# Maxima spread over the partitions by TensorE, and the projections' weights prepared apart for q, k and v

## What is computed

```python
x = x + _layernorm(attn(_layernorm(x)) )      # attn: qkv = x @ w_qkv.T + b_qkv, then per chunk:
    inter = jnp.einsum('bhcd,bhde->bhce', qb * decay_q[None, :, :, None], S)
    scores = jnp.einsum('bhcd,bhed->bhce', qb, kb) * dmask[None]
    intra = jnp.einsum('bhce,bhed->bhcd', scores, vb)
    S_new = lam_c[None, :, None, None] * S + jnp.einsum('bhcd,bhce->bhde', kb * decay_k[None, :, :, None], vb)
    # output: attn @ w_out.T + b_out
x = x + _layernorm(ffn(_layernorm(x)))        # ffn: wq = w.astype(float8_e4m3fn), y = (x @ wq) * scale
    gate = jax.nn.silu(_quantized_matmul(x, gate_w, gate_scale))
    up = _quantized_matmul(x, up_w, up_scale)
    y = _quantized_matmul(gate * up, down_w, down_scale)
```

## Time and profile before

| | us |
|---|---|
| median of 3 runs | 1037.26 |
| lowest, highest | 1037.1, 1037.28 |
| the profiled execution | 1037.88 |
| its span | 1036.1 |

### The profile page before, as it was taken

One profiled execution on the slowest core, in us unless ns is written; L12 is line 12 of the kernel. 1 busy time (PEld: TensorE's weight loads), 2 busy tenths in 40 slices (PEclk: granted clock), 3 DMA queues, 4 the chain that ended last, 5 costly groups with the idle time before them and its releaser, 6 DMA issues.

```text
span 1036.1 us, 21805 instructions
## 1 busy us (share of the span) xinstructions
PE 955.5 (92%) x8388; PEld 704.4 (68%) x8388; DVE 664.6 (64%) x1340; ACT 526.3 (51%) x997; POOL 686.2 (66%) x839
## 2 busy tenths in 40 slices
PE   1997988949988699999999999999999999999997
PEld 1775766636766486777867768677776787867774
DVE  7756767636478776666667656676666666666422
ACT  3535756535745563555635546355553555635432
POOL 2649898946765685676856768567585675856643
PEclk9998999979999899999999999999999999999999
DMA  9577989996899997494774947859477494732010
GB/s 342 142 208 196 253 203 254 214 266 180 192 194 225 204 195 143 113 184 89 147 146 110 183 88 149 152 104 184 91 145 140 115 184 94 144 69 42 26 37 21
DMA packets 297496, 159.79 MB, mean 154 GB/s; under 512 B 141616, under 2 KB 272688, under 8 KB 297264
## 3 DMA queue, kind: packets, MB, share of 16 engines
q1 hardware_dynamic: 296672, 157.86, 68.7%
q10 hardware_dynamic: 720, 0.54, 0.2%
HBM read 82.86 MB, written 41.94 MB: 120 GB/s over the span
## 4 chain that ended last, share of the span: by engine, by line
PE 48%; POOL 27%; DVE 8%; issue 8%; ACT 3%; SPq 2%; DMA 2%; POOLq 0%; DVEq 0%; ACTq 0%
PE bank L821 16%; PE bank L807 13%; PE att L784 8%; POOL att_pool L958 5%; POOL w_pool L972 4%; POOL hl L968 3%; POOL rstd L899 3%; PE bank L700 3%; PE bank L715 2%; POOL xr L964 2%; POOL rstd L903 2%; DVE stats L1206 2%; POOL vv L942 2%; DMA dram_qk<-qk_hl 2%; PE att L700 2%
## 5 line engine op out<-in xcount | busy, mean ns | idle before, releaser
L807 PE MATMUL bank<-f_pool,gate_q 128*128 128x256 f16 x1536 | 185.0, 274 | 5.4 <-DMA f_pool<-hl 4.4
L807 PE MATMUL bank<-f_pool,up_q 128*128 128x256 f16 x1536 | 183.4, 273 | 0.0
L821 PE MATMUL bank<-down_q,w_pool 128*128 128x512 f16 x768 | 168.3, 379 | 8.4 <-POOL w_pool L972 8.4
L958 POOL TENSOR_TENSOR att_pool<-p,att_pool 128x512 f16<-128x512 f32 x128 | 145.9, 1161 | 37.3 <-ACT att_pool L505 37.3
L807 PEld LDWEIGHTS bank<-f_pool,gate_q 128*128 128x128 f16 x1536 | 147.9, 98 | 26.3 <-DMA f_pool<-hl 4.6
L1337 DVE SCALAR_TENSOR_TENSOR w_pool<-bank,us_t,w_pool 128x256 f32<-128x256 f32 x192 | 84.0, 479 | 125.7 <-PE bank L807 100.1
L807 PEld LDWEIGHTS bank<-f_pool,up_q 128*128 128x128 f16 x1536 | 150.3, 98 | 17.5
L896 POOL TENSOR_TENSOR rstd<-mv,eps_t 128x1 f32<-128x1 f32 (+1 forms) x112 | 27.8, 249 | 192.4 <-DVE mv L1209 173.5
L821 PEld LDWEIGHTS bank<-down_q,w_pool 128*128 128x128 f16 x768 | 74.0, 98 | 96.7 <-issue 9.8
L972 POOL TENSOR_TENSOR w_pool<-w_pool 128x512 f16<-128x512 f32 x96 | 111.2, 1160 | 42.1 <-ACT w_pool L557 42.1
L505 ACT CAST att_pool<-p 128x512 f16<-128x512 f32 x128 | 76.7, 619 | 66.0 <-DVE p L1247 65.9
(11 more groups left out here) (139 smaller groups left out, 1800.1 us busy)
## 6 DMA issues: line engine op xcount, KB each, us to landing
xr<-in_x SPq DMA_DIRECT2D x32, 512.0 KB, 4.5
dram_qk<-qk_hl SPq DMA_DIRECT2D x64, 256.0 KB, 5.1
att_pool<-dram_qk SPq DMA_DIRECT2D x64, 256.0 KB, 6.8
f_pool<-dram_qk SPq DMA_DIRECT2D x64, 256.0 KB, 6.9
dram_v<-vv SPq DMA_DIRECT2D x32, 256.0 KB, 2.6
dram_kd<-kd_hl SPq DMA_DIRECT2D x32, 256.0 KB, 3.2
qn_pool<-dram_qk SPq DMA_DIRECT2D x32, 256.0 KB, 7.9
out_x<-w_pool SPq DMA_DIRECT2D x32, 256.0 KB, 2.1
```

The lines of the kernel that those rows point to most:

```text
L807: ins = nc.tensor.matmul(b[:, j * TOK:(j + 1) * TOK], w[:, k, o * P:(o + 1) * P], x1_hl[:, v % 2, part, k], start=(k == 0 and part == 0), ...
L821: ins = nc.tensor.matmul((b_gate, b_up)[t][:, :], h_hl[:, part, k, t * P:(t + 1) * P], down_q[:, k], start=(k == 0 and part == 0), stop=(k ...
L958: nc.gpsimd.tensor_tensor(pr_hl[:, 1, heads(g)], by_head(p32[:, g % 2]), pr_hl[:, 0, heads(g)], ALU.subtract).then_inc(p_lo_d, 1)
```

## The change

- **Loads.** x of unit 0 comes as two tiles with a semaphore each. The weights come by thirds (q, k, v; all four row blocks of 512 columns) in place of four row blocks of all columns; x of unit 1 follows the first third. The scale of the down projection is loaded by SP in `ahead(0)` and not by ACT's queue. An identity matrix (`eye_c`, float32) is a new input, in the memory of `state`; the ones lie in that of `state_d`.
- **Weights.** Bound, scale, bias and the two halves are made for each third apart. `third(w, part, half)` now takes all row blocks and 256 columns, the columns of one `project_qk(0, i)`, which waits for its own half.
- **Maxima.** POOL's two `partition_all_reduce` are gone. PE multiplies one column of maxima, broadcast over 128 columns, by the identity, so every partition has all 128 values, and DVE reduces them. For k and v these matmuls stand behind `project_qk(0, 0)` and `project_qk(0, 1)`.
- **Bound on the rows.** The 12 squares on ACT and 36 matmuls of ones are gone. DVE takes the largest absolute value of each row of a piece as it is rounded (`row_limit`), squares and adds 12 columns once (`row_sums`), and PE adds over partitions with one matmul (`sum_rows`). `norms` and `scale_h` run later: `scale_h` behind `ahead(13)`.
- **Unit loads.** `load_unit` has four steps, dealt out by `UNIT_STEPS`: unit 0 over `ahead(6)` to `ahead(9)`, unit 1 over `ahead(11)` to `ahead(13)`.

```diff
-        SUMMED = {3: (0,), 4: (1,), 5: (2,), 6: (3,), 7: (4,), 8: (5, 6), 9: (7,), 10: (8,), 11: (9,), 12: (10,),
-                  13: (11,)}
-        NORMS = {7: 0, 10: 1}
+
+        UNIT_STEPS = {6: ((0, 0),), 7: ((0, 1),), 8: ((0, 2),), 9: ((0, 3),),
+                      11: ((1, 0),), 12: ((1, 1), (1, 2)), 13: ((1, 3),)}
...
-            def load_unit(s):
+            def may_load(s):
...
+            def load_unit(s, step=None):
+                if step in (None, 0):
+                    may_load(s)
+                    load_stack(s, 1, (0, 0, 1, 1))
+                if step in (None, 1):
+                    load_stack(s, 0, (0, 1, 0, 1))
+                if step in (None, 2):
+                    load_q(s)
+                    load_v(s)
+                if step in (None, 3):
+                    load_kt(s)
...
                     sp.dma_start(bo[:, :], b_out).then_inc(wout_in, 16)
+                    sp.dma_start(ds_t[:, :], down_s).then_inc(scl_in, 16)
...
-            load_x(0)
-            for k in range(KT):
-                sp.dma_start(w_stage[:, k], w_qkv_t[k * P:(k + 1) * P, :]).then_inc(w_in[k], 16)
-            load_x(1)
+            for t in range(T):
+                sp.dma_start(xr[:, 0, t], x_u[0][:, t]).then_inc(x0_in[t], 16)
+            for part in range(3):
+                sp.dma_start(w_stage[:, :, part * D:(part + 1) * D],
+                             w_qkv_t.rearrange("(k p) n -> p k n", p=P)[:, :, part * D:(part + 1) * D]
+                             ).then_inc(w_in[part], 16)
+                if part == 0:
+                    load_x(1)
...
-                if k == LEAD - 6:
-                    load_unit(0)
-                if k == LEAD - 1:
-                    load_unit(1)
+                if k in UNIT_STEPS:
+                    for unit, step in UNIT_STEPS[k]:
+                        load_unit(unit, step)
...
-            def square(n):
-                act.wait_ge(f_q_d, n + 1)
-                at_least(act, square_mm, n - 1)
-                nc.scalar.activation(squares(n), piece_out(n), ACT.Square, scale=SQUARE).then_inc(square_d, 1)
...
-            act.dma_start(ds_t[:, :], down_s).then_inc(scl_in, 16)
-            x_normalise(0)
-            x_hi(0)
-            act.wait_ge(w_scale_d, 1)
-            for part in range(3):
-                for half in range(2):
-                    w_hi(third(wqkv_hi, part, half), third(w_stage, part, half))
+            for t in range(T):
+                act.wait_ge(rs_d[LN_X], t + 1)
+                normalised(LN_X, x_src(0)[:, t], x_src(0)[:, t], t).then_inc(nrm_d[LN_X], 1)
+                act.wait_ge(nrm_d[LN_X], t + 1)
+                nc.scalar.copy(x_half(0)[:, t, 0], x_src(0)[:, t]).then_inc(x_hi_d, 1)
+            w_hi(0)
             x_normalise(1)
             x_hi(1)
+            w_hi(1)
+            w_hi(2)
...
-                if 2 <= k < 14:
-                    square(k - 2)
...
-            def sum_squares(n):
-                pe.wait_ge(square_d, n + 1)
-                if n == 0:
-                    pe.wait_ge(eps_d, 3)
-                if n == 8:
-                    pe.wait_ge(norms_d, 1)
-                for k in range(3):
-                    ins = nc.tensor.matmul((b_gate, b_up)[n // 4 % 2][:, :], ones[:, :], squares(n)[:, k * D:(k + 1) * D],
-                                           start=(n % 4 == 0 and k == 0), stop=(n % 4 == 3 and k == 2))
-                ins.then_inc(square_mm, 1)
+            def sum_rows():
+                pe.wait_ge(eps_d, 3)
+                pe.wait_ge(row_sum_d, 1)
+                nc.tensor.matmul(b_gate[:, 0:4], ones, row_sum[:, :], start=True, stop=True).then_inc(row_sum_mm, 1)
+
+            def spread(out, col):
+                return nc.tensor.matmul(out, small[:, col:col + 1].to_broadcast([P, P]), eye, start=True, stop=True)
+
+            def spread_w_max(part):
+                pe.wait_ge(eye_in, 16)
+                pe.wait_ge(w_max, part + 1)
+                spread(b_gate[:, part * P:(part + 1) * P], part).then_inc(w_max_all, 1)
+
+            def spread_wout_max():
+                pe.wait_ge(wout_max, 1)
+                for n in range(3):
+                    ins = spread(b_up[:, n * P:(n + 1) * P], 20 + n)
+                ins.then_inc(wout_max_all, 1)
...
-                        if n == 0 and j == 0 and (i == 0 and k % 2 == 0 or i == 2 and k == 0):
-                            pe.wait_ge(w_lo_d, i + k // 2 + 1 if i == 0 else 4)
+                        if n == 0 and j == 0 and k == 0:
+                            pe.wait_ge(w_lo_d, i + 1)
...
+                if k == 2:
+                    spread_wout_max()
                 project_qk(k, 0)
+                if k == 0:
+                    spread_w_max(1)
                 project_qk(k, 1)
+                if k == 0:
+                    spread_w_max(2)
                 project_qk(k, 2)
                 project_qk(k, 3)
-                for n in SUMMED.get(k, ()):
-                    sum_squares(n)
+                if k == 12:
+                    sum_rows()
...
+            spread_w_max(0)
...
-            pool.wait_ge(w_max, 1)
-            nc.gpsimd.partition_all_reduce(small[:, 6:7], small[:, 5:6], P, RMAX).then_inc(w_max_all, 1)
...
-                if k == 1:
-                    pool.wait_ge(wout_max, 1)
-                    nc.gpsimd.partition_all_reduce(small[:, 36:39], small[:, 20:23], P, RMAX
-                                                   ).then_inc(wout_max_all, 1)
-                if k == 11:
+                if k == 12:
...
             def prepare_qkv():
...
+                                                 apply_absolute_value=True))
+                link(nc.vector.tensor_scalar(col(7, 3), col(4, 3), 1.0 / 256.0, None, ALU.mult))
+                w_limit(0, 0)
+                w_limit(0, 1)
+                x_moments(1, 0)
+                w_scale(0)
+                x_moments(1, 1)
+                scale_bias(0)
+                w_lo(0, 0)
+                w_lo(0, 1)
+                w_limit(1, 0)
+                w_limit(1, 1)
+                w_limit(2, 0)
+                w_scale(1)
+                w_limit(2, 1)
+                scale_bias(1)
+                w_lo(1, 0)
+                w_lo(1, 1)
+                w_scale(2)
+                scale_bias(2)
+                w_lo(2, 0)
+                w_lo(2, 1)
...
+            def w_limit(part, half):
+                dve.wait_ge(w_in[part], 16)
+                link(nc.vector.tensor_reduce(col(30 + 2 * part + half), w_stage[:, 2 * half:2 * half + 2,
+                                                                                part * D:(part + 1) * D],
+                                             AX.XY, ALU.max, apply_absolute_value=True))
+                if half:
+                    nc.vector.scalar_tensor_tensor(out=col(part), in0=col(30 + 2 * part), scalar=col(31 + 2 * part),
+                                                   in1=col(7 + part), op0=ALU.max, op1=ALU.max).then_inc(w_max, 1)
+
+            def w_scale(part):
+                dve.wait_ge(w_max_all, part + 1)
+                link(nc.vector.tensor_reduce(col(40 + part), b_gate[:, part * P:(part + 1) * P], AX.X, ALU.max))
+                power_of_two(col(43 + part), col(40 + part), 2.0 ** -30, 2.0 ** 35)
+                link(nc.vector.tensor_scalar(col(46 + part), col(43 + part), 2.0 ** -5, None, ALU.mult))
+                nc.vector.reciprocal(col(60 + part), col(46 + part)).then_inc(w_scale_d, 1)
...
 
             def scale_wout():
                 dve.wait_ge(wout_max_all, 1)
+                link(nc.vector.tensor_reduce(col(36, 3), b_up[:, 0:3 * P].rearrange("p (n q) -> p n q", n=3), AX.X,
+                                             ALU.max))
...
+            def row_limit(n):
+                dve.wait_ge(f_q_d, n + 1)
+                ins = nc.vector.tensor_reduce(row_max[:, n:n + 1], piece_out(n), AX.X, ALU.max,
+                                              apply_absolute_value=True)
+                ins.then_inc(row_max_d, 1)
+
+            def row_sums():
+                dve.wait_ge(row_max_d, 12)
+                link(nc.vector.tensor_reduce(col(24), row_max[:, :], AX.X, ALU.max))
+                link(nc.vector.tensor_scalar(col(25), col(24), E4M3_OVER, 0.0, ALU.mult, ALU.mult))
+                link(nc.vector.tensor_tensor(row_max[:, 0:8], row_max[:, 0:8], row_max[:, 0:8], ALU.mult))
+                link(nc.vector.tensor_reduce(row_sum[:, 0:2], row_max[:, 0:8].rearrange("p (w k) -> p w k", w=2), AX.X,
+                                             ALU.add))
+                nc.vector.tensor_scalar(row_sum[:, 2:4], row_sum[:, 0:2], 0.0, col(25), ALU.mult, ALU.add
+                                        ).then_inc(row_sum_d, 1)
+
+            def norms():
+                dve.wait_ge(row_sum_mm, 1)
+                nc.vector.tensor_scalar(col(26, 4), b_gate[:, 0:4], 1.0, None, ALU.mult).then_inc(norms_d, 1)
+                dve.wait_ge(norms_d, 1)
```

(19 more changed lines are left out.)

124 lines of the change are left out of this document (59 added, 65 removed).

## The result

| | before | after |
|---|---|---|
| median, us | 1037.27 | 1026.53 |
| lowest, highest | 1037.1, 1037.91 | 1025.97, 1027.76 |
| the profiled execution | 1037.88 | 1026.47 |
| its span | 1036.1 | 1024.7 |

The ratio is 0.9897, with a 95% interval of 0.988 to 0.9914: 10.7 us faster. 1024 was predicted, with a range of 1013 to 1034.

What follows compares the result with a forecast made beforehand. The head was taken as bound by a DVE-POOL loop, not PE. Start, 18.34 us rounds and the end put the first masked product at 277.8 for 291.02, 13.2 earlier: 1037.26 - 13.2 = 1024 us, range 1013 to 1034.

Steps and rivals of the forecast that it cites:

- The rounds: DVE's rounds in the head: 16.69 us plus 1.65 for the row-maximum reduce, behind DVE's wait, makes 18.34 us.
- T(1) to T(12): Starts of DVE's rounds 1 and 12, predicted at 44.5 and 248.7 us, with 11 rounds of 18.34 between.
- The hidden maxima: Rival for the head's rounds: the reduce's 1.65 us falls into a wait, total 1006 us; chance 8%.
- POOL's stall: Round 2: POOL's 8.11 us idle behind the second all-reduce disappears, some 10 us; rival that it stays, 1034, 5%.
- The squares: Head: dropping 12 ACTIVATEs and 36 matmuls cuts PE's unit from 16.4 to 15.7 us but gains nothing by itself.
- The unit loads: Unit 0's load in steps over ahead(6) to ahead(9) removes DVE's 10.59 us wait; steps costed at nothing.
- The start: Before the rounds: PE starts at 15.4 us, 6 gained, not reaching DVE; rival of 5 us late, 1029, 14%.
- T(0): Start of DVE's round 0, in ahead(0): predicted at 31.1 us, before 27.9.
- The spread: PE's spreading of weight maxima at the start: no profile row, bounds 0.1 and 1 us, taken as 0.4.
- The last two rounds: End of the head: DVE and POOL run free, 12.3 us each plus 1.0 for norms, ending at 274.3.
- `scale_h` and the flag: Behind the last v_sum: 2.4 us for scale_h and 1.1 for the product with ds_t, before the masked product.
- Nothing given back: From PE's first scores to the end: more than 747.1 us would give the gain back.

Runs made afterwards that it cites:

- the maxima in the wait: Changed kernel with each piece's row maximum moved behind the next piece's rounded_sum, inside DVE's wait for POOL: 1009.54 us, ratio 0.974.

## Why the prediction came out as it did

Step by step, by its own account.

- **The rounds: right.** 18.34 us predicted, 18.36 measured, and for the reason given: the reduce of f16 takes 1.74 us and stands behind DVE's only wait. By the Trainium skill (VectorE: DVE Perf Modes, The perf-mode tier table) `tensor_reduce` has the 1x mode alone; the trace agrees, 1.74 us for 1536 of f16 and 1.75 for 1536 of f32. T(1) to T(12) was 204.2 by the sum and is 203.97: DVE did wait 0.88 us for down_scale in `ahead(1)`, but inside its slack, so the 0.5 us for it did not come. The hidden maxima, a rival, would have been the truth had the reduce stood ahead of the wait, as the experiment shows.
- **POOL's stall: right**, by the run that puts it back: 9.4 us in one round. The Trainium skill (VectorE: DVE Perf Modes, Rules for kernel authors) sends a reduction along partitions to GpSimd. Here that rule loses, 9.4 us against 0.93 us on PE, though the instruction alone is only 1.12.
- **The squares: "this buys nothing by itself" was too little.** Put back, with the norms in their old places, they cost 3.7 us in one round, and the 5.9 us less from T(12) to PE's scores, which the account shows, are gone again (32.43).
- **The unit loads: right in the kernel after**, no wait of DVE for x in rounds 9 and 10. The block's price in the kernel before was not "some 10 us" but 15.4, in two rounds, and in this loop it is 4 to 5. The 7.3 us that a block may take for nothing were those of the short round: here one of 15.6 left a wait of 4.75. And late spills did hold ACT: its longest wait for one is 1.77 us in the rounds of the kernel after, but 5.16 in the squares' run. The prediction's sum uses none of these, but whoever adds up the parts gets it wrong: -13 alone, -4 to -5 beside the maxima.
- **The start: 3.0 us too cheap**, the largest miss. The step that failed is PE's start, "tile by tile they are issued some 1.5 us earlier, so 15.4": it was 17.76. The transposes were issued at 9.19, as expected, but landed 6.3 to 7.6 us after their issue and not 4.6 to 5.1; ahead of the last megabyte of weights they landed in 3.5 to 4.0. So DVE waited for the spread of k until 23.46, not 21.0, and T(0) is 33.57 for 31.1; the 10.1 us between the two were right. Part of the size is this execution's: in the seven profiled executions with this start PE's first projection begins at 16.92 to 18.93 and T(0) is 32.07 to 34.75, all later than predicted. The transposes weren't the only thing missed: where the weights came last, PE began 4.57 us behind the first spread (17.69 and 13.12 with the maxima in the wait). The other 0.5 us up to T(1) is `rounded` at 2.73 in place of 2.17, with POOL's `q_lo` and `x_lo` beside it. The spread was near the guess of 0.4: 0.46 to 0.77.
- **The last two rounds: 0.7 us too cheap** (26.3 for 25.6, from T(12) to the first instruction of `scale_h` at 277.73). PE waited for `row_sum`, which I had taken for hidden, and lost its clock for the 24 matmuls behind it, 7.03 us for 5.34. It had no pause from there to the end of unit 13, where DVE then waited 1.19 for v:

```profile
254.18 0.36 PE L693 MATMUL bank<-row_sum,state_d 128*128 128x4 f32 x2 [2.66 <-DVE row_sum L1253]
254.40 7.03 PE L742 MATMUL bank<-w_pool,o_t 128*128 128x512 f16 x24
...
277.12 0.69 DVE L1314 TENSOR_TENSOR v<-bank,bv 128x512 f32<-128x512 f32 x1 [1.19 <-PE bank L742]
```

- **`scale_h` and the flag: 1.5 us too dear.** 2.05 us for 3.5; the product with ds_t took 0.54, not 1.15.
- **Nothing given back: right**, 746.7 us for 747.1.

The misses are +3.0 (the start), -0.3 (the rounds), +0.7 and -1.5 us: the masked product is at 279.78, not 277.8, and the median at 1026.5, not 1024. The mechanism of the rounds was right. That the whole came within 2.5 us is in part luck, since terms that were 1.8 us too dear cover half of the 3.7 that were too cheap.
